# A causal attention and mixture-of-experts layer on one core: first transfers regrouped on SyncE, wider weight rows, bf16 tile tables, identity passes ahead of planned waits, and other due times for the planner

## The reference

```python
xn = _layernorm(x)
# attention, 16 heads of 16 numbers, causal
q = einsum('btc,hcd->bhtd', xn, Wq) + bq      # k and v alike
probs = softmax(q @ k.T * 16**-0.5 + causal)
y = (probs @ v) over all heads
attn = y @ Wo + bo
# experts: 8 of them, each token takes its best 2
topk_logits, selected = top_k(xn @ Wr, 2)
p = softmax(topk_logits)
for e in range(8):
    w_e = where(selected == e, p, 0).sum(-1)
    h = (clip(silu(xn @ Wg[e]), -7, 7) * (xn @ Wu[e])) @ Wd[e]
    out += h * w_e
return x + attn + out
```

## Time and profile before

| | before |
|---|---|
| runs, us | 440.17, 440.21, 441.91; median 440.21 |
| profiled execution, us | 439.97 |
| its span, first to last instruction, us | 438.2 |
| mean granted TensorE clock | 0.969 of full |
| busy: PE, DVE, ACT, POOL, us | 402.4, 335.5, 220.7, 195.6 |

### The profile page before, as it was taken

How to read it: one execution, slowest core, us unless ns; L and a number is a source line. 1 busy time by engine, 2 the same in 40 slices (tenths; PEclk the granted TensorE clock), 3 DMA queues, 4 the chain that set the end, 5 groups by cost and what they waited for, 6 DMA issues and landing times.

```text
span 438.2 us, 8403 instructions
## 1 busy us (share of the span) xinstructions
PE 402.4 (92%) x2755; PEld 224.3 (51%) x2755; DVE 335.5 (77%) x1043; ACT 220.7 (50%) x511; POOL 195.6 (45%) x224
## 2 busy tenths in 40 slices
PE   8999849886999999999999999999999999999983
PEld 8575414454436425644756477555654576455332
DVE  6917998899689596969489767688479879880795
ACT  1644353341662764455653554546456444656960
POOL 6421324673237416863684247524753354404320
PEclk9999967899899999999999999999999999999996
DMA  7369544955225524784566346616656444100772
GB/s 239 121 179 296 162 157 143 326 186 180 96 85 185 168 67 137 253 236 140 175 194 215 112 145 210 238 59 210 206 150 216 144 159 135 25 14 3 251 256 72
DMA packets 35972, 71.68 MB, mean 164 GB/s; under 512 B 7479, under 2 KB 19896, under 8 KB 35930
## 3 DMA queue, kind: packets, MB, share of 16 engines
q0 software_dynamic: 9360, 39.99, 27.9%
q1 hardware_dynamic: 23018, 27.08, 20.2%
q10 hardware_dynamic: 3552, 4.08, 3.0%
HBM read 55.85 MB, written 15.60 MB: 163 GB/s over the span
## 4 chain that ended last, share of the span: by engine, by line
PE 57%; DVE 14%; DMA 8%; SPq 7%; issue 6%; ACT 5%; POOL 3%; DVEq 0%; POOLq 0%; ACTq 0%
PE psum L1377 14%; PE psum L1340 11%; PE psum L1320 10%; PE psum L1386 8%; PE psum L1297 6%; DVE psum L1020 5%; SPq L727 5%; ACT probs L934 3%; DMA xg<-xn_rows,token 3%; DMA expert_rows<-wvr,slots 3%; PE psum L1359 2%; PE psum L1211 2%; DVE x L1076 2%; PE psum L1367 2%; DMA stage<-expert_rows 1%
## 5 line engine op out<-in xcount | busy, mean ns | idle before, releaser
L934 ACT ACTIVATE probs<-psum 128x512 f32<-128x512 f32 (+1 forms) x320 | 150.6, 580 | 44.1 <-PE psum L1320 43.6
L1020 DVE CUSTOM_DVE_ANT_0 psum<-psum,maskrow 128x384 f32<-128x384 f32 (+3 forms) x256 | 116.5, 523 | 24.0 <-PE psum L1297 23.8
L1320 PE MATMUL psum<-packq,packk 99*128 99x512 bf16 (+7 forms) x384 | 88.4, 337 | 11.3 <-DMA packq<-negt 4.7
L1023 DVE TENSOR_REDUCE mxa<-psum 128x1 f32<-128x512 f32 x128 | 79.9, 678 | 15.7 <-PE psum L1297 15.3
L1340 PE MATMUL psum<-probs,v 128*32 128x512 f32 (+3 forms) x768 | 77.7, 505 | 2.1 <-POOL probs L860 1.7
L1320 PEld LDWEIGHTS psum<-packq,packk 99*128 99x128 bf16 (+1 forms) x384 | 30.7, 98 | 73.6 <-issue 28.8
L860 POOL TENSOR_SCALAR_AFFINE_SELECT probs<-probs 128x512 f32<-128x512 f32 (+1 forms) x48 | 40.6, 845 | 48.7 <-ACT probs L934 48.4
L827 POOL DMA_INDIRECT xg<-xn_rows,token x39 | 37.6, 964 | 41.4 <-PE psum L1367 34.4
L845 POOL DMA_INDIRECT expert_rows<-wvr,slots x39 | 39.3, 1008 | 34.6 <-ACT wvr L954 22.9
L1297 PE MATMUL psum<-packk,packq 48*128 48x512 bf16 (+3 forms) x384 | 48.7, 328 | 3.5 <-DVE mxa L1023 1.5
L1377 PE MATMUL psum<-xgt,wexp 128*128 128x128 f32 x384 | 49.5, 284 | 0.6 <-DVE negt L1049 0.5
(11 more groups left out here) (121 smaller groups left out, 458.5 us busy)
## 6 DMA issues: line engine op xcount, KB each, us to landing
qk_parts<-stage SPq DMA_DIRECT2D x24, 256.0 KB, 2.8
stage<-expert_rows SPq DMA_DIRECT2D x16, 256.0 KB, 3.8
packq<-qk_parts SPq DMA_DIRECT2D x32, 96.0 KB, 2.6
packk<-qk_parts SPq DMA_DIRECT2D x28, 96.0 KB, 2.6
x<-in_x SPq DMA_DIRECT2D x4, 512.0 KB, 5.8
packq<-qk_parts SPq DMA_DIRECT2D x32, 64.0 KB, 2.0
xn_rows<-probs ACTq DMA_DIRECT2D x4, 512.0 KB, 6.4
out<-x SPq DMA_DIRECT2D x16, 128.0 KB, 2.8
```

The costliest lines, as they stand in the source:

```text
L934: act.activation(probs[:, g % RING, h, 0:width], psum[:, bank, 0:width], ACT.Exp, scale=SCALE)\
L1020: ins = dve.tensor_tensor_reduce(out=chunk, in0=chunk, in1=maskrow[:, BANK - width:], scale=1.0, scalar=NEG, op0=ALU.add, op1=ALU.max, acc ...
L1023: ins = dve.tensor_reduce(into, chunk, op=ALU.max, axis=AX.X)
L1320: ins = pe.matmul(psum[:, bank, at:at + width], packk[0:KROWS[h // UP], h // UP, u % SLOTS, j // HALF, h % UP, P * (j % HALF):P * (j % HAL ...
```

## The change

Seven things are changed together.

- The loads of the weights move from ScalarE's queue to SP's, those of the q/k weights right behind the first part of x. Their biases become four more columns of the same tensor, so one transfer with rows of 4112 bytes takes the place of two. The stores of xn to HBM move from ScalarE to SP too.
- VectorE's table `tiles` is made of bf16 operands alone, with the tiles as the middle axis; a bf16 counter table is made by POOL (`const 3`), and `place` makes one more copy, `tile_of`. The matmuls of `list` read that table with a stride of 16 elements.
- Ahead of chosen TensorE stages `hold_clock` puts identity passes. They are chosen where the planner's own model leaves TensorE idle for over 700 ns, and 70% of that gap is filled, at a planned 109 ns a pass. They write into a bank that the stage is about to fill, after it is free. There are 93: 5 ahead of `qk1 0`, 22 ahead of `s 0 0`, 4 ahead of `s 0 3`, 5, 6 and 6 ahead of `nat 0 10` to `nat 0 12`, 7, 7 and 6 ahead of `nat 1 5` to `nat 1 7`, 9 ahead of `gu 3`, 16 ahead of `proj 12`.
- The loads of unit 1 must wait, in the plan, for the first unit's first `neg`.
- `PACE`, `SPREAD`, `STAY`, `NEG_LAG` and `RATE` have other values.
- Due times of `nat`, q/k tiles, v blocks, routing and `pv` are others.
- `ln` is planned on SP, with other due times.

```diff
-STAY = 8000
-NEG_LAG = 8000
-SPREAD = 0.6
+STAY = 6400
+NEG_LAG = 6000
+SPREAD = 0.65
...
-RATE = 280
+RATE = 240
...
-PACE = dict(attention=(60000, 395000), experts=(90000, 345000))
+IDLE = 700
+HELD = 0.7
+PASS = 109
+PACE = dict(attention=(80000, 418000), experts=(76600, 358200))
...
-            return 5000 if m < EARLY else 30000 + 800 * (m - EARLY)
-        ahead = 10000 * (u == UNITS - 1)
+            return 5000 if m < EARLY else 46200 + 700 * (m - EARLY)
+        ahead = 16800 * (u == UNITS - 1)
...
-    job("ACT", ("weights_qk",), 950, [("SP", ("x", 1))], due=-50, lag=2000, size=540000)
-    job("ACT", ("weights_v",), 2200, [("ACT", ("weights_qk",))], due=-50, lag=2000, size=820000)
+    job("SP", ("weights_qk",), 500, due=-11, lag=2000, size=526336)
+    job("SP", ("weights_v",), 1900, due=-9, lag=2000, size=820000)
...
-        job("ACT", ("ln", q), 420, [("DVE", ("ln", q)), ("SP", ("load", 0, 0, 0))], due=34000 + q, lag=2000, size=524288)
+        job("SP", ("ln", q), 500, [("DVE", ("ln", q)), ("SP", ("load", 0, 1, len(RUNS) - 1))], due=200 + q, lag=2000, size=524288)
...
-        due = 10 * n + 6 + op if k < 4 else 25000 + 1500 * (k - 4)
+        due = 10 * n + 6 + op if k < 4 else 29400 + 3000 * (k - 4)
...
-        due = 10000 + 600 * t
+        due = 4700 + 1100 * t
...
+                if u == 1:
+                    after += [("DVE", ("neg", 0))]
...
+def passes_before():
+
+    held, end = {}, PLANNED.start["PE", ORDER["PE"][0]]
+    for stage in ORDER["PE"]:
+        begin = PLANNED.start["PE", stage]
+        if begin - end > IDLE and fills_of(stage):
+            held[stage] = int(HELD * (begin - end) / PASS)
+        end = begin + PLANNED.jobs["PE", stage][0]
+    return held
...
+            def load_qk_weights():
+                sp.dma_start(wqkb[:, :], wqk_d).then_inc(wqk_in, 16)
...
-                low, high = digits[:, k, :, 0, :], digits[:, k, :, 1, :]
-                shape = [P, NT, MAX_TILES]
-                chain(route_step, dve.tensor_tensor(low, iota_t[:, :].unsqueeze(1).to_broadcast(shape),
-                                                    postile[:, k, :].unsqueeze(2).to_broadcast(shape), ALU.is_equal))
-                dve.tensor_tensor(high, low, high_digit[:, :].unsqueeze(2).to_broadcast(shape), ALU.mult)
+                low, high = digits[:, k, 0, :, :], digits[:, k, 1, :, :]
+                shape = [P, MAX_TILES, NT]
+                chain(route_step, dve.tensor_tensor(low, iota_tiles[:, :, :], tile_of[:, k, :].unsqueeze(1).to_broadcast(shape), ALU.is_equal))
+                dve.tensor_tensor(high, low, high_digit[:, :].unsqueeze(1).to_broadcast(shape), ALU.mult)
...
+            def hold_clock(stage):
+
+                if stage in HOLDS:
+                    bank, _ = wait_room(pe, fills_of(stage)[0])
+                    for _ in range(HOLDS[stage]):
+                        pe.transpose(psum[:, bank, 0:P], ident[:, :], ident[:, :])
```

More of the change, by code:

```diff
@@ L318, in make_plan @@
         w = k // 2
-        due = 10 * n + 6 + op if k < 4 else 25000 + 1500 * (k - 4)
-        after = [("ACT", ("xnt", 2 * b + n, c)) for c in range(DC)] + [("ACT", ("weights_qk",))]
+        due = 10 * n + 6 + op if k < 4 else 29400 + 3000 * (k - 4)
+        after = [("ACT", ("xnt", 2 * b + n, c)) for c in range(DC)] + [("SP", ("weights_qk",))]
         pe(("qk1", k), 853, after, due=due, takes=("qk", k))
@@ L331, in make_plan @@
     for t in range(NT):
[L332 to L333 removed]
+        due = 4700 + 1100 * t
+        pe(("v", t), 884, [("ACT", ("xnt", t // 4, c)) for c in range(DC)] + [("SP", ("weights_v",))] + ([("DVE", ("v_ones",))] if t == 0 else []),
            due=due, takes=("v", t))
@@ L342, in make_plan @@
     for r in range(2):
[L343 to L346, removed]
+        dve(("top", r), 620, [("ACT", ("v", TB * (r + 1) - 1))], 39100 if r else 26)
+        dve(("topi", r), 1180, [("DVE", ("top", r))], 39101 if r else 27)
+        dve(("hot", r), 520, [("DVE", ("topi", r))], 39102 if r else 28)
+    job("ACT", ("gates",), 216, [("DVE", ("topi", 1))], 39101)
     pe(("route",), 1400, [("DVE", ("hot", 1))], 100, takes=("route",), mode="b")
-    dve(("place",), 3700, [("PE", ("route",))], 20003, frees=("route",))
+    dve(("place",), 3700, [("PE", ("route",))], 39103, frees=("route",))
     for k in range(2):
-        dve(("rows", k), 2300, [("DVE", ("place",))], 20004)
-        dve(("tiles", k), 2950, [("DVE", ("place",))], 20004)
+        dve(("rows", k), 2300, [("DVE", ("place",))], 39104)
+        dve(("tiles", k), 2200, [("DVE", ("place",)), ("POOL", ("const", 3))], 39104)
     pe(("list",), 2600, [("DVE", ("rows", 1)), ("DVE", ("tiles", 1))], 100, takes=("list",), mode="b")
-    dve(("experts",), 1600, [("DVE", ("tiles", 1))], 20005)
-    dve(("list",), 1300, [("PE", ("list",))], 20006, frees=("list",))
+    dve(("experts",), 1600, [("DVE", ("tiles", 1))], 39105)
+    dve(("list",), 1300, [("PE", ("list",))], 39106, frees=("list",))
     dve(("gates",), 750, [("ACT", ("gates",))], 30000)
-    dve(("widen",), 228, [("DVE", ("v_ones",)), ("DVE", ("ln", 3)), ("ACT", ("weights_v",))], 12000)
+    dve(("widen",), 228, [("DVE", ("v_ones",)), ("DVE", ("ln", 3)), ("SP", ("weights_v",))], 12000)
     pe(("bias",), 853, [("DVE", ("widen",))], 30000, takes=("bias",))
@@ L410, in make_plan @@
             after = [("POOL", ("mask", g))]
-        pe(("pv", g), width * 4 / 2.4 + 45, after + ([("ACT", ("v", TB * (u // G + 1) - 1))] if n == 0 and u % G == 0 else []), due_at[g + 1] - 100,
+        pe(("pv", g), width * 4 / 2.4 + 45, after + ([("ACT", ("v", TB * (u // G + 1) - 1))] if n == 0 and u % G == 0 else []), due_at[g + 1] + 1600,
            ("y", u, c) if js[0] == 0 else None, "c")
@@ L438, in make_plan @@
         due = m0 + (m1 - m0) * i / MAX_TILES
-        after = [("DVE", ("list",)), ("ACT", ("ln", 3))] if i == 0 else []
+        after = [("DVE", ("list",)), ("SP", ("ln", 3))] if i == 0 else []
         if i >= 2:
@@ L675, in wait_heads, with walk @@
             eng.wait_ge(heads_ready, 2 * (u // 2) + c + 1)
-        def walk(engine, stages):
+        def walk(engine, stages, before=None):
             for kind, *args in ORDER[engine]:
+                if before:
+                    before((kind, *args))
                 stages[kind](*args)
@@ L757, in store_out @@
                 sp.dma_start(out_d[P * t:P * (t + 1), :], x[:, t, :]).then_inc(out_done, 16)
-            walk("SP", {"x": load_x, "ones": spread_ones, "store": store, "load": load, "neg": neg_rows, "z_load": load_z, "out": store_out})
+            walk("SP", {"x": load_x, "weights_qk": load_qk_weights, "weights_v": load_v_weights, "ones": spread_ones, "ln": store_xn, "store": store, "load": load, "neg": neg_rows, "z_load": load_z, "out": store_out})
             sp.wait_ge(out_done, 16 * NT)
```

75 lines of the change are left out of this document (43 added, 32 removed).

## The result

The changed kernel takes 422.0 us (median of 4 runs, 421.39 to 422.84) against 441.06 us for the kernel before (4 runs, 440.17 to 441.93): ratio 0.9569, 95% interval 0.9538 to 0.9601. The profiled execution took 421.39 us, its span is 419.6 us.

The account below looks back on a forecast made before the run. TensorE was taken as the bound from 110.5 to 426.5 us, so gains were sought in the other stages. Terms -2.9 - 1.5 + 0.8 - 2.5 - 1.5 - 1.5 = -9.1 gave 431.0 us median, 8 in 10 between 425.5 and 439.5.

Parts of the forecast that it names:

- A: End: expert sums finish before the last weighing of v, so the last block's transposition no longer waits; -2.9 us.
- B: End: passes keep the clock at 2.4 GHz for the last four projections; -1.5 us.
- C: Front, up to the first exponential: six DMAs freed from unit 1's loads, but a later maxima copy; +0.8 us, bounds -0.3, +3.
- D: Front, first exponential to token list's end: weighing runs at full clock; -2.5 us, bounds -0.4 and -4.
- E: First expert tile: its gather stands behind one fetch and a subtraction instead of two fetches; -1.5 us.
- F: Third stage, up to the fourth score step at 110.5: passes remove half-clock time; -1.5 us.
- the middle: Fourth score step to the end of the last weighing of v: new order forecast at 0, bounds -3 and +3 us.
- Rival 3: Middle loses density: each of 39 expert tiles makes TensorE wait 0.4 us longer; 446.7 us, chance 0.11.
- the stride: List matmuls in the front reading their table strided: priced at nothing, bounds 0 and twice their 1.35 us.
- rows 10: Profile rows of 60 passes alone, 7 begun in one microsecond, 11 in one five later; taken as passes raising the clock.
- rival 2: Passes don't hold the clock, so the gains resting on it mostly go; 436.2 us, chance 0.08.

Follow-up runs that it names:

- e5_new_middle: Kernel before with only five planner numbers of the middle taken from the changed kernel (STAY, SPREAD, paces, weighted values' due time, last unit's maxima): 428.96 us, ratio 0.9722.
- e1_no_passes: Changed kernel without its 93 identity passes, every engine's order the same: 426.89 us, ratio 0.9647.
- e9_token_major: Changed kernel with its bf16 list tables laid token by token, so VectorE writes and the list matmuls read adjacent elements: 420.4 us, ratio 0.9539.
- e2_list_packed: Changed kernel with the bf16 tile tables stored in the old order: list matmuls read adjacent elements, VectorE writes through a strided view: 429.1 us, ratio 0.9721.
- e18: Changed kernel itself, measured again on the same chip as the version with planner numbers found by trying: 421.45 us, ratio 0.9565.

## Why the prediction was right or wrong

| step | forecast, us | measured, us | from |
|---|---|---|---|
| A and B, the end | -4.4 | -4.7 | 11.74 to 7.06 behind the last weighing |
| C, first exponential | +0.8 | -0.7 | 60.65 to 59.91 |
| D, to the list's end | -2.5 | +1.3 | 11.90 to 13.22 |
| E, to the first tile's transposition (82.85, now 83.26) | -1.5 | -0.2 | 10.30 to 10.13 |
| F, to the fourth score step | -1.5 | -2.6 | 27.70 to 25.14 |
| the middle | 0 | -11.8 | 315.91 to 304.14 |

**The step that failed** is "a new order of the same matmuls can neither win nor lose much", and with it "The order of the middle: 0, bounds -3 and +3 from its 9.5 us of idling". The middle gave 11.8 us, and TensorE idled there for 4.64 us, less than the 7 to 13 that were to show the forecast right. The prediction took TensorE's busy share as its pace. The same matmuls were busy 305.45 us in one order and 299.50 in the other, so the busy time holds waits too; the profile only models where a pipelined matmul ends. The waits were to be seen in the profile before, at the weight loads of the scores, 31.5 us of them, and the prediction doesn't use them. Rival 3 had seen that the order decides, but only with a loss.

Outside the middle the parts sum to -6.9 us against the -9.1, with D and E missed and C and F better than forecast: that they come near it is partly luck.

**A and B** were right in mechanism and sum. A alone is about 2.4 (the 9.33 us of `e5_new_middle`, which has no passes, against 11.74), B 2.1 (`e1_no_passes`).

**C.** The copy came at 50.71 instead of 51.5, and from it to the first exponential took 9.2 us instead of 10.0. The result lies below my lower bound of -0.3.

**D.** The list's start came 2.8 us earlier, 2.1 of it behind the first exponential, close to the -2.5. What I priced at nothing, the stride, took 3.4 us, above my upper bound of twice 1.35.

**E** failed: the gather landed as late with one fetch ahead of it as with two. Unit 1's loads, which moved behind the six DMAs, issue from 56.44 on and share the DMA engines (share 0.84 in the third stage, 0.66 before); that they are the cause was not tested. The clock is not: it was 0.78 in this stretch of the changed kernel and 1.00 in that of `e9_token_major`, which is as long (10.54 us, from 72.22 to 82.76).

**F** was right in mechanism and under-sized: the granted clock of this stretch rose from 0.90 to 1.00, and without the passes it takes 27.8 us at 0.81. Passes do hold the clock, but rows 10 show it only by the pace: their clock reads 1.00 in both microseconds, as the trace has no clock record before 6.03 us. What shows it is `e1_no_passes`. With the passes' part of D, the forecast gave the passes 5.2 us in all (rival 2 against the forecast); without them the time rises by 4.9.

## What to carry to other kernels

A TensorE that is 97% busy in a stage can still lose nearly 4% there to the order of the queues: read what its weight loads wait for, line by line, before pricing a new order at nothing. When a planner sets the order, a number in it has no price of its own; time several sets, and expect neighbours to lie 4 to 8 us apart in 422. When two engines hold the same banks, shortening one can hand most of the wait to the other; cut both in one experiment before ruling the cause out.

## What the runs showed of the hardware

The middle of the changed kernel is rigid while the granted clock is 1.00. For this one order it took 304.13, 304.24, 304.13, 304.31 and 304.11 us (after, `e1`, `e2`, `e9`, `e18`), though it began at 108.40, 111.59, 116.05, 107.92 and 108.58.

A moving operand (the one that streams through TensorE) in bf16 read with a stride of 16 elements made 32 matmuls of 78 columns take 4.74 us in the changed kernel, where the clock fell on the way, and 4.75 us in `e1_no_passes` at 1.00 throughout. With adjacent elements they took 1.34 us at 1.00 (`e9_token_major`) and 2.24 us at 0.50 (`e2_list_packed`). TensorE was busy all the while in the strided ones, and yet the granted clock fell from 2.4 to 1.2 GHz during them (single microseconds of the changed kernel: length, busy time and matmuls of TensorE, clock, DMA share, GB/s). In `e1_no_passes` it fell right behind them, at 74.1 us.

```profile
69.00:70.00 1.00, 1.00 (x9) 1.00 0.71 209
70.00:71.00 1.00, 1.00 (x9) 0.84 0.57 186
71.00:72.00 1.00, 1.00 (x9) 0.50 0.17 55
```

With the adjacent table of `e9_token_major` the clock stayed at 1.00 from 60 to 90 us, with TensorE busy for only 7.05 of the 10 us from 70 to 80.
